# Rotation partners taken by a vector shuffle in two cross attentions, and block-turned maxima, sums and values in self attention

## The reference

```python
# cross attention of layer 0; H = 16 heads of D = 16
q = (x_q @ W_q).reshape(B, Tq, H, D).transpose(0, 2, 1, 3)
k, v = kv[..., :C], kv[..., C:]                     # kv = x_kv @ W_kv
x1, x2 = x[..., ::2], x[..., 1::2]                  # _rotate, of q and of k
x1p, x2p = x1 * cos - x2 * sin, x1 * sin + x2 * cos
att = einsum('bhqd,bhkd->bhqk', q, k) / sqrt(D); att = softmax(where(mask, att, -1e9))
y = einsum('bhqk,bhkd->bhqd', att, v); return y.transpose(...).reshape(B, Tq, C) @ W_c
# cross attention of layer 1: as above, but x1, x2 = x[..., :half], x[..., half:],
# a bias on every projection, and only keys of the last 128 positions up to the query
# self attention of layer 1; 16 heads of 64
qkv = X @ W_qkv; q, k, v = qkv[..., 0], qkv[..., 1], qkv[..., 2]
weights = softmax(einsum('bqhd,bkhd->bhqk', q, k) / 8)
return einsum('bhqk,bkhd->bqhd', weights, v).reshape(b, s, h * d) @ W_out
```

## Time and profile before

| | us |
|---|---|
| median of three runs | 2953.72 |
| lowest and highest of them | 2947.42, 3137.99 |
| the profiled execution, its own time | 2952.82 |
| its span, first to last instruction | 2951.0 |
| PE busy in the span | 2658.3 (90%) |
| DVE, ACT, POOL busy | 1945.2, 1399.1, 1107.2 |

### The profile page before, as it was taken

One profiled execution on the slowest core, in us unless ns is written; L12 is line 12 of the kernel. 1 busy time (PEld: TensorE's weight loads), 2 busy tenths in 40 slices (PEclk: granted clock), 3 DMA queues, 4 the chain that ended last, 5 costly groups with the idle time before them and its releaser, 6 DMA issues. The chain is left out here.

```text
span 2951.0 us, 51682 instructions
## 1 busy us (share of the span) xinstructions
PE 2658.3 (90%) x17628; PEld 1631.8 (55%) x17629; DVE 1945.2 (66%) x3269; ACT 1399.1 (47%) x2199; POOL 1107.2 (38%) x854
## 2 busy tenths in 40 slices
PE   7997899999868899999999999999889999857998
PEld 4775333333235556565656565656544454456997
DVE  4776777877668765657575656666546666574555
ACT  2433466666558653434343434343335555443333
POOL 3233323233036343435343434343443333063333
PEclk9998799999879999999999999999989999958999
DMA  5002222222111000000000000000043232146666
GB/s 163 0 0 63 61 59 61 58 61 58 30 58 44 1 1 1 1 1 1 1 1 1 1 1 1 1 1 1 1 113 81 74 79 69 37 138 230 219 211 195
DMA packets 102982, 160.60 MB, mean 54 GB/s; under 512 B 28349, under 2 KB 63432, under 8 KB 97160
## 3 DMA queue, kind: packets, MB, share of 16 engines
q1 hardware_dynamic: 97784, 147.88, 17.5%
q0 software_dynamic: 3408, 8.46, 0.8%
q10 hardware_dynamic: 1600, 1.61, 0.2%
HBM read 91.79 MB, written 14.96 MB: 36 GB/s over the span
## 5 line engine op out<-in xcount | busy, mean ns | idle before, releaser
L1678 DVE TENSOR_REDUCE self_nmax<-self_SM 128x2 fp32r<-128x1024 f32 x256 | 313.3, 1224 | 211.7 <-PE self_SM L1567 211.7
L1656 ACT ACTIVATE self_PT<-self_ST 128x1024 f32<-128x1024 f32 x256 | 262.9, 1027 | 329.4 <-PE self_ST L1592 329.4
L1723 POOL TENSOR_TENSOR self_U<-self_PT 128x1024 f32<-128x1024 f32 x64 | 153.9, 2405 | 613.5 <-ACT self_PT L1656 613.5
L499 DVE TENSOR_REDUCE cross_nmax<-cross_S 128x2 f32<-128x1024 f32 x256 | 310.7, 1222 | 110.2 <-PE cross_S L347 109.2
L444 ACT ACTIVATE cross_PT<-cross_S 128x1024 f32<-128x1024 f32 x256 | 260.0, 1023 | 123.3 <-PE cross_S L358 121.4
L1726 POOL TENSOR_TENSOR self_U<-self_U,self_PT 128x1024 f32<-128x1024 f32 x128 | 303.4, 2371 | 31.9 <-ACT self_PT L1656 27.0
L1602 PE MATMUL self_W<-self_PT,self_V 128*64 128x512 f32 x1024 | 237.4, 606 | 19.6 <-ACT self_PT L1656 14.6
L1146 DVE TENSOR_REDUCE cross_nmax<-cross_S 128x4 f32<-128x1024 f32 x128 | 156.5, 1223 | 133.4 <-PE cross_S L967 133.3
L1698 DVE RECIPROCAL self_rcp<-self_W 128x512 f32<-128x512 f32 x64 | 214.7, 3354 | 33.8 <-PE self_W L1609 33.1
L1083 ACT ACTIVATE cross_PT<-cross_S 128x1024 f32<-128x1024 f32 x128 | 131.0, 1024 | 127.6 <-PE cross_S L983 127.4
L1602 PEld LDWEIGHTS self_W<-self_PT,self_V 128*64 128x64 f32 x1024 | 72.5, 139 | 161.4 <-issue 123.2
(11 more groups left out here) (450 smaller groups left out, 7002.8 us busy)
## 6 DMA issues: line engine op xcount, KB each, us to landing
moe_staged<-in_L_ffn_W SPq DMA_DIRECT2D x36, 1024.0 KB, 6.1
cross_ks<-cross_parts SPq DMA_DIRECT2D x384, 64.0 KB, 2.3
cross_qs<-cross_parts SPq DMA_DIRECT2D x376, 64.0 KB, 2.3
all_x<-in_L_ffn_W SPq DMA_DIRECT2D x14, 1024.0 KB
all_x<-sorted_rows SPq DMA_DIRECT2D x83, 130.0 KB, 2.1
cross_cT<-in_ctx_T SPq DMA_DIRECT2D x16, 512.0 KB, 4.6
sorted_rows<-all_spare_row SPq DMA_DIRECT2D x1, 5460.0 KB, 23.8
all_x<-in_x SPq DMA_DIRECT2D x8, 512.0 KB, 4.0
```

The source lines that it names most:

```text
L499: dve.tensor_reduce(nmax[:, g % 2, 0:R, n % PER_G], S[:, slot[st], :, :], AX.X, ALU.max, negate=True).then_inc(s_maxed, 1)
L1656: act.activation(PT[:, k, :, :], ST[:, :, :], ACT.Exp).then_inc(exped.sem, 1)
L1678: dve.tensor_reduce(nmax[:, i, 0:P:D], SM[:, :, :], AX.X, ALU.max, negate=True).then_inc(maxed.sem, 1)
L1723: pool.tensor_tensor(U[:, c % 2, :, :], PT[:, 0, :, :], PT[:, 1, :, :], ALU.add).then_inc(added.sem, 1)
```

## The change

**Cross attentions.** The weights' columns are reordered outside the kernel (`spread_order(paired)`) so that a row's rotation partner is always 16 partitions away inside a block of 32 (`PARTNER`). The `rot` product, its bank and the load of `turnm` go; VectorE makes the partner rows with a shuffle from `rows` in SBUF to `rsin` and multiplies in place. `rot` is no step of TensorE any more. The table `at` moves the halves of `v` and `out`: in cross0 to single places among the projections, with `mt` ahead by 0.7 unit, and in cross1 one unit apart, the first where `rot` stood.

**Self attention.** The maxima go into `nmax`, 32 columns, which VectorE transposes in blocks of 32 x 32; eight DMAs of SyncE, each 4 x 32 numbers, put them on the two rows of a now double `mrow`. `ma` and `mb` go. VectorE transposes the `sum` (block-wise, 128 x 512), takes the reciprocal of 16 columns of it, transposes the values too (in place of ScalarE's copy), multiplies, and transposes the product back to `OT`. `av` waits for each exponential where it needs it.

```diff
-        for m, ts in enumerate(((-14.4, -12.8), (1.6, 3.2))):
+        for m, ts in enumerate(((-4.5, -1.5), (3.5, 6.5))):
             for part, t in enumerate(ts):
                 at[("v", b, m, part)] = o + t
...
-        for m, ts in enumerate(((41.6, 42.0), (43.2, 43.25))):
+        for m, ts in enumerate(((43.5, 46.5), (51.5, 54.5))):
...
-    RINGED = ("norm", "qk", "rot", "v", "out", "mt")
+    RINGED = ("norm", "qk", "v", "out", "mt")
...
-                elif kind == "rot":
-                    dst = free_bank(st)
-                    pe.wait_ge(s_act, nth_act[("qk", b, n, KC - 1)])
-                    if b == 0:
-                        pe.wait_ge(s_rot, 48)
-                    pe.matmul(dst, turnm[:, :], rows[:, n % 2, :], start=True, stop=True).then_inc(s_full, 1)
...
                 elif kind == "rot":
                     if b == 0:
-                        dve.wait_ge(s_rot, 48)
-                    dve.wait_ge(s_full, nth_full[st])
+                        dve.wait_ge(s_rot, 32)
+                    dve.wait_ge(s_act, nth_act[("qk", b, n, KC - 1)])
...
-                    dve.tensor_tensor(rsin[:, n % 2, :], src, sin[:, :], ALU.mult).then_inc(s_dve, 1)
+                    dve.stream_shuffle(rsin[:, n % 2, :], rows[:, n % 2, :], PARTNER).then_inc(s_shuffled, 1)
+                    dve.wait_ge(s_shuffled, nth_rot[st])
+                    dve.tensor_tensor(rsin[:, n % 2, :], rsin[:, n % 2, :], sin[:, :], ALU.mult).then_inc(s_dve, 1)
...
                 if k < NT - 1:
                     add("max", (c + 1) * NT + k + 1, NC * NT)
+                if k == NT - 2:
+                    add("rows", c + 1, NC)
...
-                    add("ma", c + 1, NC)
-                    add("mb", c + 1, NC)
...
                     if k == 0:
                         reach(pe, drained["dve"], "dve", b, order, ("k", c, rel))
-                        reach(pe, drained["act"], "act", b, order, ("mb", c, rel))
+                        rows_in(pe, b, order, c, rel)
...
                 elif kind == "av":
-                    exped.wait(pe, b, NT * (n + 1))
                     dst = free_bank(pe, b, order, st)
...
                     for k in range(NT):
+                        exped.wait(pe, b, NT * n + k + 1)
...
+                elif kind == "rows":
+                    maxed.wait(dve, b, n_max)
+                    rowed.wait(dve, b, MROWS * n_rows)
+                    n_rows += 1
+                    dve.transpose(nmax_T[:, :].bitcast(F32), nmax[:, :].bitcast(F32)).then_inc(turned_max.sem, 1)
...
-                    dve.reciprocal(rcp[:, :], bank_of(order, st)).then_inc(done, 1)
+                    dve.transpose(turned[:, :, :].rearrange("p c x -> p (c x)"), bank_of(order, st)).then_inc(done, 1)
+                    reach(dve, drained["dve"], "dve", b, order, st)
+                    dve.reciprocal(rcp[:, :], turned[:, :, 0]).then_inc(inverted.sem, 1)
+                elif kind == "av":
+                    valued.wait(dve, b, n + 1)
+                    weighed.wait(dve, b, n - 1)
+                    dve.transpose(turned_av[:, n % 2, :, :].rearrange("p c x -> p (c x)"), bank_of(order, st)).then_inc(lifted.sem, 1)
                 elif kind == "scale":
-                    reach(dve, drained["dve"], "dve", b, order, ("sum", n, rel))
+                    inverted.wait(dve, b, n + 1)
                     lifted.wait(dve, b, n + 1)
-                    dve.tensor_tensor(OT[:, n, :], Oraw[:, n % 2, :], rcp[:, :], ALU.mult).then_inc(scaled.sem, 1)
+                    scaled.wait(dve, b, n)
+                    dve.tensor_tensor(turned[:, :, :], turned_av[:, n % 2, :, :], rcp[:, :].unsqueeze(2).to_broadcast([P, NB, BLOCK]),
+                                      ALU.mult).then_inc(weighed.sem, 1)
+                    weighed.wait(dve, b, n + 1)
+                    dve.transpose(OT[:, n, :], turned[:, :, :].rearrange("p c x -> p (c x)")).then_inc(scaled.sem, 1)
...
+        def sync_steps(sp, b, order):
+            for kind, n, rel in order.steps:
+                if kind == "rows":
+                    turned_max.wait(sp, b, order.nth["rows"][(kind, n, rel)])
+                    to = mrow[:, n % 2, :].bitcast(F32).rearrange("p (i a y) -> p i a y", i=NT, y=32)
+                    for j in range(2):
+                        for a in range(P // 32):
+                            from_ = 32 * a + NT * j
+                            sp.dma_start(to[j * D:j * D + 1, :, a, :], nmax_T[from_:from_ + NT, :].bitcast(F32)).then_inc(rowed.sem, 16)
```

165 lines of the change are left out of this document (84 added, 81 removed).

## The result

| | us |
|---|---|
| changed kernel, median of four runs | 2983.86 |
| kernel before, beside it | 2950.57 |
| ratio, 95% interval | 1.0093 [1.0069, 1.0117] |
| profiled execution after: span, mean granted clock | 2982.6, 0.936 (before: 2951.0, 0.957) |

The ratio leaves out the one execution of before that took 3137.99 us, in a slower state of the chip, and isn't the quotient of the two medians (1.011).

A forecast was written before the change was run, and what follows sets the result against it. The prediction took TensorE to bound the kernel, with VectorE second. Self attention +1, cross0 -25, cross1 -7 and the cross attentions' starts +2 on 2952.8 gave 2924 us, 1.0% faster; own range 2905 to 2945, 8 in 10 within 2862 to 2978.

The forecast's parts named there:

- Cross0, -25, range 0 to -33: Cross0: TensorE spared rot, gaining 3.1 us a batch over eight, -25 us, from 0 to -33.
- the whole 4.1: Cross0: four rot products' TensorE time a batch, 4.1 us; upper bound for slot waits, taken as 1 us.
- Self attention, +1: Self attention: DMA issuing takes the place of the time saved; 0 - 2 + 3 = +1 us, from -60 to +67.
- the chain 15.3: Self attention: from one column step's first exact through maxima, transposition and eight DMAs to the next's, 15.3 us.
- the -0.2 that I took: Self attention, batch end: transpositions added around scale, long reciprocal and ma gone; -1 to +1 us a batch, taken as -0.2.
- The 14.3 us that TensorE alone was to need: Self attention: TensorE's time per column step without the DMA chain, 14.3 us, about 99.8 for seven.
- rival 1: Self attention: issuing is short, so all that TensorE is spared is gained, -58 us; 2865 us, chance 0.2.
- The start was priced at +3: Self attention: the very first column step has no period to hide its DMAs in, +3 us once.
- Cross1, -7: Cross1: TensorE's cover waits for VectorE's reduction behind the shuffle; gain 0.2 by 32 rotations, -7 us, from 0 to -34.
- +2 was meant for both cross attentions: Starts of both cross attentions: two VectorE operations in a row and cos one load earlier, +2 us, from -1 to +4.
- Rival 3: Self attention: slower through the DMA chain, one issue 0.84 us, period 16.5; 2991 us, chance 0.12.
- Rival 4: Cross0: VectorE takes over, and nothing of cross0's and cross1's gains is left; 2956 us, chance 0.11.

The follow-up runs named there:

- cosine_by_shuffle: Changed kernel with GpSimd's cosine product in cross0 released by the shuffle instead of the sine product behind it; 2983.94 us, ratio 1.0086.
- cross1_rot_later: Changed kernel with cross0's cast 2 units later and four mrow DMAs, plus cross1's rotation and cast one unit later; 2864.71 us, ratio 0.9703.
- old_table: Changed kernel with cross0's old due times for v, out, mt, norm and statistics, keeping the shuffle; 2967.16 us, ratio 1.0044.

## Why the prediction was wrong, step by step

**What bounds.** "VectorE is second with 79%", and so I looked for the counterpart of the gain on VectorE alone. It was ScalarE, at 63% and idle between its operations, because its queue holds operations that wait for GpSimd. The busy share didn't show that. The group of the cast did, in the trace of before: 22.8 us of waiting for GpSimd in 360 us of cross0, just short enough to cost TensorE 4.

**Cross0, -25, range 0 to -33: the step that failed.** The range left out a loss: "no row bounds it but zero and the whole 4.1". What was missing is a term for the chain copy, shuffle, sine product, GpSimd's work, cast. Measured from the start of the copy to that of the cast: 9.1 us before and 9.7 after, by the 0.74 us shuffle and its hand-over. ScalarE reached the cast 6.7 us after the copy before (449.56 less the wait of 2.44, from 440.44) and 6.5 after; and there TensorE now has bare units of 1.67 us (446.10, 447.76, 449.43), since the extra steps lie elsewhere. So TensorE ran ahead of a chain that had become longer. That chain and place are the cause is shown both ways: later by one and two units wins 45 and 62 us, and sooner by one loses 46 us in the kernel before. The run with the old table splits the loss in another way: the shuffle with its chain turns the -33 us of the inner part into +4, and the new places of `v` and `out` add 28. How each splits between the longer chain and the faster TensorE is argued from these rows, not shown; shortening the chain by 0.3 us (cosine_by_shuffle) won nothing that its runs could tell.

The two sizes that I did price were right: 0.74 us for a shuffle (0.74 measured), and 25.5 us of gain for 25 in the inner part once the wait is gone, with VectorE at 89%. That the whole of cross0 then gains 39.7 I had not seen: its end, with the new places of `out`, no longer runs at a lower clock, 12.5 us that I had no term for.

**The clock, no term at all.** TensorE's rows showed 1.00 in cross0 before, and I priced every wait by its own length. Behind the wait of 2.66 us TensorE ran at 0.50 for some 10 us, nearly twice the time for each product. Between the changed kernel and the one with the late cast this is 34.0 of 57.5 us, the difference in TensorE's busy time for the same instructions; the other 23.5 are the waits themselves.

**Self attention, +1: right, with its mechanism.** The rival to beat was 58 us of gain from TensorE, and the DMA chain ate it: -0.5 us. The terms: one issue 0.67, measured 0.61; transposition 0.20, measured 0.21; the chain 15.3, measured 14.75. The 0.5 us that this is better went again: one or two column steps of most batches take 16.3 us with a stretch at a lower clock, and the products `out` at a batch's end wait 14.9 us in all for `OT` where they waited 7.0 (one of these is in the earlier trace rows), +1 us a batch for the -0.2 that I took. The 14.3 us that TensorE alone was to need were right too: 14.2 measured with four DMAs, where it is free, and rival 1 comes true to 3 us. The start was priced at +3, and the stretch to the first `OT` took 4.2 us more.

**Cross1, -7: the mechanism right, the size wrong.** The cover waits for the reduction behind the shuffle. Its groups, before and after:

```profile
L954 PE MATMUL cross_S<-cross_band,all_ident_bf 64*64 64x512 bf16 x1024 | 85.9, 394 | 8.3 <-ACT cross_PT L1083 4.6 <-DVE cross_nmax L1146 2.7
```

```profile
L956 PE MATMUL cross_S<-cross_band,all_ident_bf 64*64 64x512 bf16 x1024 | 91.4, 401 | 25.1 <-DVE cross_nmax L1142 19.3 <-ACT cross_PT L1079 4.6
```

First to last `out` is 303.0 us for 303.2: all but nothing is left of what TensorE was spared. From the first `wq` to the first `out`, the start, it took 2.7 us more, where +2 was meant for both cross attentions.

**Rival 3** (slower) had the wrong part, and its price of an issue, 0.84 us, wasn't met. **Rival 4** had the right part and the wrong engine; it ended at 2956, where the real chain went on to 2984, since it stopped at "nothing is left".

## What to carry to other kernels

- When an engine that bounds gets faster, list what stands in the other engines' queues with a wait inside, and for each how long its input takes and how long the queue now takes to come to it. A wait that costs nothing today is slack that has been used up; look for it in the groups' idle times, not in the busy shares.
- Price a new wait of TensorE at more than its length: ask if the rows behind such waits show a lower clock. The waits of the old table, 1.6 us at most in a batch once its start is past, were followed by far less of it than those of 2.66 and 2.06 us with nearly the same sum (52.9 and 57.8 us idle); `v` and `out` stand elsewhere in the two kernels, so the length of the waits is not shown to be the only reason.
- Count the DMAs of a chain, not their bytes: one DMA to two rows cost no more than one to a single row, and half the number freed 55 us.
- Moving one step in one queue moves what other queues wait for: the same fault came back in cross1 when a cast was moved there (cross1_rot_later).

## What of the hardware was not expected

- The granted clock of TensorE fell to 0.50 behind each of the six waits of 2.65 to 2.69 us of the changed kernel in cross0, for 3 to 14 us, but behind only three of its six of 2.00 to 2.07. In old_table it fell behind two of the six waits of 1.57 to 1.61 us (7 us each), and in cosine_by_shuffle behind all of those of 1.76 to 1.78. What decides it isn't settled by these runs.
- GpSimd's 128 x 512 product took 1.73 us beside a VectorE product of two SBUF inputs and 1.28 alone; VectorE's 128 x 256 product took 1.80 us beside a GpSimd addition that ran for 2.37 us, and 0.43 alone.
- Issuing a small DMA on SyncE took 0.57 us by the median with four rows and 0.50 with eight.
